# Two changes of order in an eight-core layernorm, attention and FFN block: the layernorm's queue order and copy width, and two attention slots side by side

## What is computed

```python
xn = _layernorm(x)
qkv = xn @ w_qkv                      # 32 query heads, 8 key and value heads of 128
xq, xk = _apply_rope(xq), _apply_rope(xk)
scores = einsum('bhsd,bhtd->bhst', xq, keys) / sqrt(128)    # causal
attn = softmax(scores) @ values
ffn = (silu(xn @ w_gate.T) * (xn @ w_up.T)) @ w_down.T      # inner width 11008
out = x + attn @ w_o + ffn
```

## Time and profile before

| | us |
|---|---|
| runs shown | 9265.19 and 9499.78, median 9382.49 |
| profiled execution | 8857.74 |
| its span, core 0, the slowest | 8856.2 |
| spans of the other cores | 8774.3 to 8850.5 |
| layernorm passes, core 0 | 0 to 640 |
| Q, K and V projections | 640 to 2340 |
| attention | 2360 to 4000 |
| output projection, FFN, final stage | 4000 to 8856 |

### The profile page before, as it was taken

The page is one execution under the profiler, slowest core; times in us unless marked ns, Lnnn a source line. Parts: engine busy times, 40 slices in busy tenths (PEclk is TensorE's granted clock), DMA queues, the critical chain, the costliest instruction groups (busy, mean ns, idle before and its releaser), DMA issues.

```text
span 8856.2 us, 72371 instructions; the slowest of 8 cores (8774.3 to 8856.2 us)
## 1 busy us (share of the span) xinstructions
PE 7075.1 (80%) x29510; PEld 2963.1 (33%) x30080; DVE 1566.0 (18%) x2332; ACT 1031.6 (12%) x1198; POOL 469.6 (5%) x594
## 2 busy tenths in 40 slices
PE   2229977887787887777979988989798898989772
PEld 1124433333221111113434434434343443434331
DVE  4433311111122222220000010110101011010221
ACT  3430000000133333330000000000000000000000
POOL 0110000000000000000000010000101001010110
PEclk9999988898887877878989999989899999999885
DMA  7985455444300000005543375563837556483886
GB/s 211 207 166 95 88 141 142 140 131 140 94 10 11 10 10 10 10 6 128 114 111 77 77 119 92 96 111 67 137 76 111 94 92 112 79 134 74 124 142 203
DMA packets 390469, 884.59 MB, mean 100 GB/s; under 512 B 84865, under 2 KB 261122, under 8 KB 361730
## 3 DMA queue, kind: packets, MB, share of 16 engines
q0 software_dynamic: 106464, 530.62, 34.6%
q1 hardware_dynamic: 273954, 332.53, 13.2%
q10 hardware_dynamic: 9728, 16.78, 0.7%
HBM read 1007.78 MB, written 226.49 MB: 139 GB/s over the span
## 4 chain that ended last, share of the span: by engine, by line
PE 70%; DMA 14%; DVE 8%; issue 4%; ACT 3%; POOL 0%; SPq 0%; DVEq 0%; ACTq 0%; POOLq 0%
PE PM L797 14%; PE PM L805 13%; PE PM L505 10%; PE ptr L870 9%; DMA U<-w_dT 7%; PE PM L722 5%; PE PM L420 5%; PE pl L590 4%; PE ptr L584 4%; PE PM L628 4%; DVE recip L666 2%; DVE stat L253 2%; DMA U<-x_own 2%; PE pbc L670 1%; ACT U L638 1%
## 5 line engine op out<-in xcount | busy, mean ns | idle before, releaser
L870 PE MATMUL ptr<-AR,U 128*128 128x512 bf16 x5393 | 1298.0, 402 | 262.2 <-DMA U<-w_dT 252.3
L797 PE MATMUL PM<-AR,U 128*128 128x512 bf16 x5394 | 1221.5, 382 | 170.7 <-DMA U<-w_guT 113.1
L805 PE MATMUL PM<-AR,U 128*128 128x512 bf16 x5395 | 1209.3, 379 | 5.7
L505 PE MATMUL PM<-U 128*128 128x512 bf16 x4010 | 962.7, 402 | 145.8 <-DVE AR L395 70.3
L870 PEld LDWEIGHTS ptr<-AR,U 128*128 128x128 bf16 x5504 | 558.0, 102 | 1001.3 <-issue 432.6
L797 PEld LDWEIGHTS PM<-AR,U 128*128 128x128 bf16 x5504 | 541.0, 98 | 825.4 <-issue 184.8
L805 PEld LDWEIGHTS PM<-AR,U 128*128 128x128 bf16 x5504 | 538.5, 98 | 649.4
L505 PEld LDWEIGHTS PM<-U 128*128 128x128 bf16 x4096 | 417.4, 103 | 682.1 <-issue 253.9
L638 ACT ACTIVATE U<-PM 128x1024 bf16<-128x1024 f32 x576 | 582.9, 1023 | 509.0 <-PE PM L628 508.9
L878 DVE COPY U<-ptr 128x512 f32<-128x512 f32 x512 | 353.9, 692 | 1204.5 <-PE ptr L870 1009.4
L826 DVE TENSOR_TENSOR AR<-PM,U 128x512 bf16<-128x512 f32 x172 | 119.0, 692 | 2436.2 <-PE PM L805 2436.2
(11 more groups left out here) (47 smaller groups left out, 2466.4 us busy)
## 6 DMA issues: line engine op xcount, KB each, us to landing
U<-w_guT POOLq DMA_DIRECT2D x86, 2048.0 KB, 14.4
U<-xnT_full_d SPq DMA_DIRECT2D x256, 512.0 KB, 3.4
y_d<-U POOLq DMA_DIRECT2D x256, 512.0 KB, 6.7
U<-w_dT POOLq DMA_DIRECT2D x96, 704.0 KB, 12.0
U<-x_full SPq DMA_DIRECT2D x16, 2048.0 KB, 18.7
AR<-x_full SPq DMA_DIRECT2D x16, 2048.0 KB, 18.2
xnT_full_d<-AR POOLq DMA_DIRECT2D x32, 1024.0 KB, 28.7
U<-w_q POOLq DMA_DIRECT2D x32, 1024.0 KB, 8.3
```

Source lines behind the costliest of these rows:

```text
L505: (lambda u=u, ht=ht, hl=hl, cpar=cpar: lambda e: e.matmul(pm[u][:, :], wkv[:, ht * 512 + u * 128: ht * 512 + (u + 1) * 128], xnf[cpar][:, ...
L797: (lambda ht=ht, rb=rb, bg_=bg_, par=par: lambda e: e.matmul(bg_[:, 0:RB], wgu[par][:, ht * 128:(ht + 1) * 128], xnA[:, ht, rb * RB:(rb + ...
L805: (lambda ht=ht, rb=rb, bu_=bu_, par=par: lambda e: e.matmul(bu_[:, 0:RB], wgu[par][:, HT * 128 + ht * 128:HT * 128 + (ht + 1) * 128], xnA ...
L870: (lambda itl=itl, rb=rb, bank=bank, u=u, par=par, inter_slot=inter_slot: lambda e: e.matmul(bank[:, 0:RB], wd[par][:, (u * SBmax + itl) * ...
```

## The change

In `ln_pass`, the part of iteration t for tile u = t-1 up to the affine is emitted ahead of the load and the statistics of tile t; transposes, copies and store of tile u come after these. The transposes go in four rounds of eight, each filling a whole slot, with one copy of 1024 columns each. Each round waits for the half of the affine that it needs.

In the attention, slots are taken in pairs, (0,1), (2,3), (4,5), (6,7), as lane 0 and lane 1. Each lane has one half of `PM`, two of now four `pbuf`, one `ptrF` bank and one partition of `pl` (0 or 64). PE's order in the loop is: scores of lane 0, PV block of lane 1 for the step before, scores of lane 1, PV block of lane 0 for the step before. Lane 1 has two steps fewer and ends first. After both lanes the two tails are emitted, lane 0 and then lane 1. The waits for the mask and for the PV and row sum banks move from the first PV matmul to the first scores. Stage buffers and `onesb` move in U3; `recip` is twice as wide.

```diff
@@ ln_pass, for t in range(ntiles + 1)
-            if t < ntiles:
-                ... load of tile t, eight bn_stats
             if t >= 1:
                 u = t - 1
                 ... bn_aggr, rstd, negmr, affine in two halves
+            if t < ntiles:
+                ... load of tile t, eight bn_stats
+            if t >= 1:
+                GW = min(8, HT)
                 dfn = dst_of(u)
-                for ht0 in range(0, HT, 4):
-                    slot = (ht0 // 4) % 2
+                for ht0 in range(0, HT, GW):
+                    slot = (ht0 // GW) % 2
                     esem, eval_ = kb._ptr_evac[slot]
                     kb.wait("tensor", esem, eval_)
-                    kb.wait("tensor", "sS", hready[ht0 + 3])
-                    for k in range(4):
+                    for k in range(GW):
+                        kb.wait("tensor", "sS", hready[ht])
                         ... transpose
-                                   ptr[:, slot * 1024: slot * 1024 + 512]
+                                   ptr[:, slot * 1024: slot * 1024 + GW * 128]
@@ attention, for each g
-        for s in range(SL):
-            for bb in range(Tn // 2):
-                ... scores, exp, mask; if pend is not None: emit_pvl(...)
-            emit_pvl(g, s, Tn, PVB, pend)
-            ... reciprocal, broadcast, copy, multiplication, store
+        for j in range(SL // 2):
+            sA, sB = 2 * j, 2 * j + 1
+            TA, TB = c["T"][sA], c["T"][sB]
+            pend = {0: None, 1: None}
+            for bb in range(TA // 2):
+                pend_new_a = emit_scores(0, g, sA, par, bb, TA)
+                if pend[1] is not None:
+                    emit_pvl(1, g, TB, pend[1])
+                    pend[1] = None
+                if bb < TB // 2:
+                    pend[1] = emit_scores(1, g, sB, par, bb, TB)
+                if pend[0] is not None:
+                    emit_pvl(0, g, TA, pend[0])
+                pend[0] = pend_new_a
+            if pend[1] is not None:
+                emit_pvl(1, g, TB, pend[1])
+            if pend[0] is not None:
+                emit_pvl(0, g, TA, pend[0])
+            emit_tail(0, g, sA)
+            emit_tail(1, g, sB)
```

`emit_scores` and `emit_tail` hold the instructions that stood in the loop over s, with these differences:

```diff
+        pb_ = 2 * lane + (bb % 2)
+        if bb == 0:
+            kb.wait("tensor", "dM", dm)
+            kb.wait("tensor", "vS", kb._pe_pv_guard[lane])
+            kb.wait("tensor", "vS", kb._pe_pl_guard[lane])
...
-                           pl[0:1, :], onesb[:, 0:1],
+                           pl[64 * lane:64 * lane + 1, :], onesb[:, 0:1],
...
+    def emit_tail(lane, g, s):
+        pv_done = kb.val("tS")
+        kb.wait("vector", "tS", pv_done)
+                       recip[0:1, lane * 512:(lane + 1) * 512],
+                       pl[64 * lane:64 * lane + 1, :]))(), inc="vS")
```

More of the change, by code:

```diff
@@ L352, in pb_dst @@
         kb.wait("vector", f"dXF{st_}", kb._pb_st[st_])
-        return lambda ht0: stg3[st_][:, ht0:ht0 + 4, :]
+        return lambda ht0: stg3[st_][:, ht0:ht0 + min(8, HT), :]
     def pb_store(u, evs):
@@ L552, in build_program @@
     maskbuf = U1[:, 0:SL * 4 * 512]
-    NP = 3
-    pbuf = [U3[:, i * 1024:(i + 1) * 1024] for i in range(NP)]
-    stage = [U3[:, 3072 + i * 512:3072 + (i + 1) * 512] for i in range(2)]
-    onesb = U3[:, 4096:4112]
+    pbuf = [U3[:, i * 1024:(i + 1) * 1024] for i in range(4)]
+    stage = [U3[:, 4096 + i * 512:4096 + (i + 1) * 512] for i in range(2)]
+    onesb = U3[:, 5120:5136]
     dm = kb.dma("sync", lambda e: e.dma_start(
@@ L572, in emit_pvl @@
+    def emit_pvl(lane, g, Tn, pend):
         tts, pb_, mg, ex = pend
@@ L589, in emit_pvl @@
             lm = kb.op("tensor",
-                       (lambda tt=tt, pb_=pb_, k=k, Tn=Tn: lambda e: e.matmul(
-                           pl[0:1, :], onesb[:, 0:1],
+                       (lambda tt=tt, pb_=pb_, k=k, Tn=Tn, lane=lane: lambda e: e.matmul(
+                           pl[64 * lane:64 * lane + 1, :], onesb[:, 0:1],
                            pbuf[pb_][:, k * 512:(k + 1) * 512],
@@ L595, in emit_pvl @@
         kb._pe_p_guard[pb_] = (lm, mg)
+    def emit_tail(lane, g, s):
+        pv_done = kb.val("tS")
+        kb.wait("vector", "tS", pv_done)
+        rc = kb.op("vector",
+                   (lambda lane=lane: lambda e: e.reciprocal(
+                       recip[0:1, lane * 512:(lane + 1) * 512],
+                       pl[64 * lane:64 * lane + 1, :]))(), inc="vS")
+        kb._pe_pl_guard[lane] = rc
+        kb.wait("tensor", "vS", rc)
+        kb.wait("tensor", "sS", kb._pe_pbc_guard)
+        bc = kb.op("tensor",
+                   (lambda lane=lane: lambda e: e.matmul(
+                       pbc[:, :], onesr[:, :], recip[0:1, lane * 512:(lane + 1) * 512],
+                       start=True, stop=True))(), inc="tS")
+        kb.wait("scalar", "tS", bc)
+        cp = kb.op("scalar", lambda e: e.copy(bcs[:, :], pbc[:, :]), inc="sS")
+        kb._pe_pbc_guard = cp
+        spar = (g * SL + s) % 2
+        kb.wait("vector", "sS", cp)
+        kb.wait("vector", f"dA{spar}", kb._pe_stage_guard[spar])
+        dv = kb.op("vector",
+                   (lambda spar=spar, lane=lane: lambda e: e.tensor_tensor(
+                       stage[spar][:, :], ptrF[lane][:, :], bcs[:, :], ALU.mult))(),
+                   inc="vS")
+        kb._pe_pv_guard[lane] = dv
+        kb.wait("sync", "vS", dv)
+        stv = kb.dma("sync",
+                     (lambda g=g, s=s, spar=spar: lambda e: e.dma_start(
+                         out=attnT_d.rearrange("h p r -> p h r")[:, g * GP:(g + 1) * GP,
+                                                                 s * 128:(s + 1) * 128],
+                         in_=stage[spar][:, :].rearrange("p (h q) -> p h q", h=GP)))(),
+                     f"dA{spar}")
+        kb._pe_stage_guard[spar] = stv
     for g in range(NKVH):
@@ L691, in build_program @@
+        if not hasattr(kb, "_qg_used"):
+            kb._qg_used = {}
+        kb._qg_used[par] = kb.val("tS")
     kb.barrier()
```

168 lines of the change are left out of this document (63 added, 105 removed).

## The result

| | us |
|---|---|
| runs of after | median 8997.31, lowest 8697.72, highest 9222.95 (11 runs) |
| runs of before beside them | median 9289.71, lowest 8845.64, highest 9746.47 (10 runs) |
| after over before | 0.986, 95% interval 0.981 to 0.991 |
| profiled execution | 8776.5, its slowest core 8774.1 (core 2) |

The change makes the kernel 1.4% faster, between 0.9 and 1.9%. Most executions of both kernels show a lower mean clock on the four cores of one die or of both and take up to 9746 us; the ratio is made from the others alone, 8846 to 8862 us for before and 8698 to 8752 for after. The prediction's two profiled figures, 8753 after 8857.7, were a ratio of 0.988. Its absolute forecast, 9277 with a range of 9175 to 9390, missed the measured 8997: it was hung on the median of two runs of before, 525 us above the profiled execution, and in after the median lies 221 us above it.

What follows compares the result with a forecast made beforehand. TensorE for most of the span; in the layernorm, its loop with DMA almost full behind it. Layernorm 65 plus attention 40 made 105 us: profiled 8857.7 to 8753, or median 9382.5 to 9277; range 9175 to 9390.

Steps and rivals of the forecast that it cites:

- What bounds the layernorm: Layernorm before: a closed loop over DVE, ACT and PE of 15.2 us sets the pace, with DMA nearly full behind it.
- Layernorm, the order: Layernorm loop: affine and next tile's statistics run side by side, shrinking it from 15.2 to 9.4 us a tile.
- Layernorm, what holds it: Layernorm: DMA stands behind the shorter loop, so only its idle time can go; gain 65 us, bounds 20 to 118.
- No queue gets a new wait: Layernorm transfers: four x and four staging buffers remain, and the load of tile t+4 is issued after the affine as before.
- DVE waiting for x_full: Sign in the layernorm pass over x_full: DVE waits for its loads, at about 14.5 us a tile with DMA at 1.0.
- The first rival: Layernorm: DMA is not the limit and the loop runs at 9.4 us; 232 + 40 = 272 us, 2.9% faster; chance 10%.
- Attention: Attention in 32 pairs: one restart instead of two, two tails in a row, step still 1.69 us; gain 40 us.
- The slower rival: Attention: lane 1's row sums at partition 64 cost x more each, 512 x added; at 0.38 us, 90 us slower; chance 6%.
- The second rival: Layernorm and attention: neither part gives anything, 0 to 20 us, about 9372 us; chance 13%.
- The later stages: Projections and FFN, 6,600 us, carried over unchanged; the prediction is wrong if they move by more than 20 us.
- The sum: Whole kernel: 65 us from layernorm plus 40 from attention, 105 us or 1.2% faster.
- The absolute time: Whole kernel: the median of 9382.5 us keeps its difference to the profiled execution, giving 9277 us.

Runs made afterwards that it cites:

- e2: The kernel before with only the attention of after (slots in pairs); ratio to before 0.9996 (0.994 to 1.005), profiled 8896.9 us.
- e4: The kernel before, in its order, with only the width changed: rounds of eight transposes and copies of 1024 columns; profiled 8769.5 us.
- e5: After with xnT_full_d laid out by tile, so a store writes 128 pieces of 8 KB instead of 4096 of 256 bytes; lowest time 8596 us.
- e9: After with the stores of e5, row sums on 128 rows and attention as one flat stream; ratio to before 0.884, lowest run 7774.95 us.
- e6: After with row sums on 128 rows, without broadcast and copy, and scores no longer behind the tails; 9157.6 us at mean clock 0.80 to 0.81.
- e3: e1 with rounds of four transposes and copies of 512 columns, so only the layernorm order differs from before; profiled 8732.5 us.
- e1: The kernel before with only the layernorm of after (order and copy width); ratio to before 0.989 (0.986 to 0.993), profiled 8733.7 us.

## Why the prediction was right or wrong

- **What bounds the layernorm.** Right that the loop set the pace; wrong that "on this core DMA has almost nothing left behind it". A share of 1.00 was read as a capacity. That 207 GB/s asked equal 208 GB/s seen is no proof of either, since bytes per turn over time per turn is the rate whatever holds the loop. What shows the loop is that the chain of the earlier trace rows fills its 15.2 us without a wait for a transfer, and that both passes of before wait for transfers no more than 15.4 us; and the same core shows a share of 0.75 in e2, with the same rate and length. Core 2's 0.73 was the warning, and it was put away with the argument that the slowest core counts. But core 0's layernorm ended only 6 us later than core 2's.
- **Layernorm, the order.** Right. Affine and statistics run beside each other, ACT's copy took 1.01 us (1.02 assumed) and DVE's 0.69 (0.7), and the loop 9.17 us (9.35).
- **Layernorm, what holds it.** This step failed: "With the same busy time per byte only the idle time can go". Busy time per byte isn't fixed; the engines moved 301 GB/s in x_own and 214 to 255 in x_full, and in e4 the pass got shorter by the loop's own 52 us whether the share in x_full was 0.76 or 1.00. The term was 65 us, measured 96 to 133 a core, over its upper bound of 118 on cores 0 and 1. The period in x_own is 9.2 us and not 10.5 to 11, and in x_full 12.4 and not 14.5 on core 0 (its 32 stores are issued from 114.2 to 498.6 us). That is on the near side of "wrong if x_full runs under 12 us a tile on core 0", so the sign that was named wouldn't have caught this.
- **"No queue gets a new wait."** Wrong. GpSimd's queue waits 320 us to issue, ACT and DVE 131 and 119 for staging buffers. "DVE waiting for x_full", the sign that was named, isn't there. That the x buffers and the staging buffers remain four was noted and not reckoned with: at 15.2 us a tile four buffers cover 61 us, at 9.4 only 38, with a store that lands after 28.7 us and 40 when more is asked of it.
- **The first rival, DMA is not the limit** (10%), had the diagnosis for before right, and the gain wrong: 232 us were not reached, since the stores took over. The Trainium skill, "DMA: Bandwidth & Descriptors", Specifications, was cited there with both halves, some 358 GB/s for a core and pieces of at least 512 bytes for full rate. The runs agree with both: 214 to 255 GB/s in x_full with 256-byte stores, 325 with 8 KB in e5, both on core 0. In e9's stretch from 135 to 210 us it is 359 on core 0. With long pieces the rival's 232 us come nearly true: 653 to 431 is 222 on core 0. The prediction said of the two rules that "no row here parts the two" and gave the pair 10%; the bound that the second one makes should have been a case of its own.
- **Attention.** 40 us forecast; 33 to 44 on six cores of after (42 on core 0) and 29 to 38 on the same six of e2. Cores 5 and 6, whose stage took 1658 us before, gained 13 and 22, and 12 and 14 in e2. Tail 12.7 us (12.6), second reciprocal 7.1 behind the first, clock back 7.9 us after the scores (8.1), second scores held 0.7 us by the multiplication, step 1.69, granted clock 0.81 (0.82). The absolute figure, 1575 to 1620, was off because it took the stretch 2360 to 4000 for the stage; by its matmuls the stage of before is 1679 us long on core 0, and 1637 after.
- **The slower rival**, row sums at partition 64, is out: on both lanes a row sum follows its PV matmul by 0.31 us, so x is 0. The Trainium skill, "TensorEngine Tiling (Array Packing)", Key Properties, says that a change of tile alone doesn't drain the array, and the trace agrees.
- **The second rival**, nothing gained, is out by the interval.
- **The later stages** moved by more than 20 us on some cores: Q projection +58 on core 2, FFN -23 on core 0. The prediction carried them over unchanged. Of the 111 us between the 193 us of core 0 and the 82 between the two slowest cores, the Q projection of core 2 makes 56 and its FFN 15; its layernorm, 31 us longer than core 0's, and its attention, 7 longer, make most of the rest.
- **The sum.** 105 us forecast, 8857.7 x (1 - 0.986) = 124 by the ratio (77 to 171 by its interval). By stages the two changed parts gave 110 to 175 us a core, 141 in the mean: a layernorm term some 40 too small, an attention term about right. That the ratio came out so near, 0.986 for 0.988, is in part luck (the two profiled executions alone give 0.991), since the slowest core of before gained most and others became the slowest, at a lower clock in a stage that the change leaves alone. That it stays within 2% was right.
- **The absolute time.** This step failed too, and it alone puts 8997 outside the range: "the difference in us carries over and gives 9277". It carried the 525 us by which the median of two runs lay above the profiled execution; over ten runs of before that distance is 432, over the runs of after it is 221. It belongs to the executions that happened to be taken and not to the kernel. By the measured ratio the base of 9382.5 would have given 9251, inside the range.

## To carry to other kernels

A busy share of DMA engines is no capacity. Add up the chain of engine work in one turn of the loop; when it fills the period and holds no wait for a transfer, the loop is the bound whatever the share says. The rate decides nothing, since it is bytes per turn over time per turn with either bound. When a loop gets shorter, redo the count of buffers for every transfer with landing time over buffers, the stores too. Ends of pieces of work (tails) are worth their full length when nothing runs beside them. Two lanes in step gave 40 us here, both reciprocals first another 105 to 125; from after, row sums that need no broadcast gave 420, and a stream that lets the next piece's first steps run across the end another 380. And a forecast in absolute time needs a base whose spread is known: two runs that differ by 2.5% are none.

## What the hardware showed that I had not expected

- DMA's busy share and landing time differ between executions and cores with the same rate: 0.71 to 1.00 and 8.1 to 36.4 us, all at 203 to 208 GB/s, in the x_full pass with before's loop. From 240 to 480 us it goes by neighbours: in before cores 0, 1, 4 and 5 have 0.98 to 1.00 and the others 0.74 to 0.88, in e4 cores 2 and 3 have 0.98 and 1.00 and the others 0.74 to 0.91, in e2 all have 0.71 to 0.76. What sets it stays open.
- GpSimd stands at the issue of a store of 4096 pieces while three others are under way, and goes on 0.31 us after the first of them has landed; an issue of 4096 pieces takes it 1.69 us, one of 128 pieces 0.53.
- A matmul with a single output row is dearer than one with 128: each change from one to the other costs about 0.09 us (0.31 against 0.22).
- A pair of cores, 2 and 3 in after, 6 and 7 in e2, had 0.81 to 0.82 of the clock for 300 us and more of dense matmuls while the others had 1.00. The Trainium skill, "TensorE: Matmul & The Clock Gate", Seeing it yourself, tells of a level of 13/16 that takes a whole die while three of its cores run dense matmuls. The size agrees; that it takes the whole die doesn't, for here two cores had it and the two beside them, with the same matmuls, had 1.00. In the kept traces it comes to the pairs 0 and 1, 2 and 3, 4 and 5, 6 and 7, and the two cores of a pair enter it within 10 us of each other; the profiled execution of before doesn't have it at all. e6 had it on all eight, but from 499 us on for one pair and only from 1958 for another. The mean clocks of executions without a trace do fit whole dies (0.80 on cores 4 to 7 in one of e3).
- The attention of before takes 1658 us on some cores and 1676 to 1681 on most, and so it does in e1 and e3, where one core each lies between. That is half of what the pairs gain, and its cause stays open.
- The rows of a reciprocal on DVE cost nothing: 3.35 us for 1x512 and 3.36 for 128x512.
